# Loading each adjacency chunk of a two-layer GNN kernel by sixteen DMAs of four row blocks in place of four DMAs of a whole quadrant

## What is computed

```python
A = adj + eye(4096)                      # layer 0
d = rsqrt(sum(A, axis=1))
A_hat = A * d[:, None] * d[None, :]
x1 = layernorm(x + elu((A_hat @ x) @ w))
out = layernorm(x1 + relu((adj @ x1) @ W.T + b))   # layer 1
```

## Time and profile before

| | |
|---|---|
| runs | 949.61, 950.19, 953.15 us (median 950.19) |
| span of the profiled execution, first to last instruction | 945.9 us |
| median less that span (lies around it) | 4.3 us |
| TensorE busy / VectorE / ScalarE / GpSimd | 798.6 / 736.0 / 530.9 / 101.9 us |
| read from HBM | 185.2 MB |
| DMAs of `adj` / of `x` | 336 of 512 KB / 64 of 128 KB |

### The profile page before, as it was taken

One profiled execution on the slowest core, in us unless ns is written; L12 is line 12 of the kernel. 1 busy time (PEld: TensorE's weight loads), 2 busy tenths in 40 slices (PEclk: granted clock), 3 DMA queues, 4 the chain that ended last, 5 costly groups with the idle time before them and its releaser, 6 DMA issues. The chain is left out here.

```text
span 945.9 us, 10551 instructions
## 1 busy us (share of the span) xinstructions
PE 798.6 (84%) x3524; PEld 656.8 (69%) x3524; DVE 736.0 (78%) x537; ACT 530.9 (56%) x1192; POOL 101.9 (11%) x108
## 2 busy tenths in 40 slices
PE   0151756569989999999999999999999999999993
PEld 0041635457768888888888888888887778888882
DVE  0454636579979878989898898988987979888861
ACT  2153535367777764475676757667573665455352
POOL 0000000000000000021110211202110231122020
PEclk9995777788999999999999999999999999999997
DMA  9999999999999999998999999999999799998900
GB/s 215 221 219 221 221 220 220 221 225 238 228 230 227 203 206 216 208 219 180 199 209 197 201 207 193 212 191 220 195 211 212 171 211 209 219 219 181 198 23 22
DMA packets 191972, 190.08 MB, mean 201 GB/s; under 512 B 6960, under 2 KB 191920, under 8 KB 191920
## 3 DMA queue, kind: packets, MB, share of 16 engines
q1 hardware_dynamic: 187312, 185.23, 96.2%
q10 hardware_dynamic: 4608, 4.20, 1.5%
HBM read 185.20 MB, written 4.19 MB: 200 GB/s over the span
## 5 line engine op out<-in xcount | busy, mean ns | idle before, releaser
L710 PE MATMUL acc<-a_hi,v_hi 128*128 128x512 f32 x1024 | 411.7, 402 | 35.6 <-DVE a_lo L496 31.4
L343 ACT ACTIVATE a_hi<-turned 128x1024 fp32r<-128x1024 f32 x256 | 265.2, 1058 | 309.5 <-DVE turned L479 151.6
L711 PE MATMUL acc<-a_lo,v_hi 128*128 128x512 f32 x1024 | 406.3, 397 | 0.0
L712 PE MATMUL acc<-a_hi,v_lo 128*128 128x512 f32 x1024 | 406.0, 396 | 0.0
L479 DVE STREAM_TRANSPOSE turned<-raw 128x2048 f32<-128x2048 f32 x128 | 294.1, 2305 | 85.2 <-DMA raw<-in_adj_dram 78.6
L496 DVE TENSOR_TENSOR a_lo<-turned,a_hi 128x1024 fp32r<-128x1024 f32 x256 | 301.4, 1215 | 23.4 <-ACT a_hi L343 15.0
L710 PEld LDWEIGHTS acc<-a_hi,v_hi 128*128 128x128 f32 x1024 | 197.3, 193 | 80.3 <-issue 28.7
L712 PEld LDWEIGHTS acc<-a_hi,v_lo 128*128 128x128 f32 x1024 | 196.9, 192 | 42.3
L711 PEld LDWEIGHTS acc<-a_lo,v_hi 128*128 128x128 f32 x1024 | 197.4, 193 | 40.7
L353 ACT ACTIVATE acc<-raw 128x256 f32<-128x256 f32 x236 | 86.8, 368 | 47.1 <-DMA raw<-in_adj_dram 47.1
L503 DVE TENSOR_REDUCE deg_parts<-raw 128x10 f32<-128x2560 f32 (+4 forms) x32 | 78.1, 2444 | 27.0 <-DMA raw<-in_adj_dram 27.0
(11 more groups left out here) (43 smaller groups left out, 347.3 us busy)
## 6 DMA issues: line engine op xcount, KB each, us to landing
raw<-in_adj_dram SPq DMA_DIRECT2D x336, 512.0 KB, 10.4
x_row<-in_x_dram SPq DMA_DIRECT2D x64, 128.0 KB, 9.3
out_dram<-normed ACTq DMA_DIRECT2D x32, 128.0 KB, 2.7
w_sb<-in_L_gnn_w_dram SPq DMA_DIRECT2D x1, 256.0 KB, 12.4
normed<-in_L_gnn_W_dram SPq DMA_DIRECT2D x1, 256.0 KB, 10.7
b_sb<-in_L_gnn_b_dram SPq DMA_DIRECT2D x1, 128.0 KB, 10.1
```

Source lines behind the costliest of these rows:

```text
L343: nc.scalar.activation(a_hi[u % 2][:, part, :], turned[u % 2][:, part, :], ACT.Copy).then_inc(s_hi, 1)
L710: pe.matmul(dst, v_hi[:, k, ch], a_hi[u % 2][:, t, :], start=begin, stop=False)
L711: pe.matmul(dst, v_hi[:, k, ch], a_lo[u % 2][:, t, :], start=False, stop=False)
L712: ins = pe.matmul(dst, v_lo[:, k, ch], a_hi[u % 2][:, t, :], start=False, stop=end)
```

## The change

A constant `BLOCKS = 4` is added. A chunk is now loaded by sixteen DMAs, each of one quadrant and four of its row blocks: 32 partitions x 4 blocks x 1 KB = 128 pieces, 128 KB. The outer loop runs over the blocks, the inner one over the quadrants 0, 2, 1, 3. The pieces are the same 1 KB, the bytes the same; `raw_loaded` waits for 256 instead of 64 a chunk. `load_x`, the weights and every other engine's instructions are as before.

```diff
+    BLOCKS = 4
@@
         def load_chunk(eng, n, qs):
             _, row, panel, _ = chunks[n]
-            for q in qs:
-                eng.dma_start(raw[buffer_of[n]][B32 * q:B32 * (q + 1), :, :], adj_part(row, panel, q)).then_inc(s_raw[buffer_of[n]], 16)
+            for first in range(0, RB, BLOCKS):
+                some = slice(first, first + BLOCKS)
+                for q in qs:
+                    eng.dma_start(raw[buffer_of[n]][B32 * q:B32 * (q + 1), some, :],
+                                  adj_part(row, panel, q)[:, some, :]).then_inc(s_raw[buffer_of[n]], 16)
@@
         def raw_loaded(eng, n):
-            eng.wait_ge(s_raw[buffer_of[n]], 64 * filled[n])
+            eng.wait_ge(s_raw[buffer_of[n]], 16 * STRIPES * (RB // BLOCKS) * filled[n])
```

## The result

The changed kernel takes 912.07 us (median of 4 runs, 908.08 to 914.45) against 951.67 us for the kernel before (with a fourth run, 949.61 to 953.61): ratio 0.959, 95% interval 0.956 to 0.962. It is faster, and by twice what was forecast: 39.6 us in place of 19 to 20. The predicted range began at 914 us, 2 us above the measured median.

A forecast was written before the change was run, and what follows sets the result against it. Loads were taken to bound groups 0 to 4, and TensorE the time after 313 us. Savings of 16.1 us there, 3 us in groups 5 to 7 and 1 us in B and C made 19 to 20 us: 931 us, range 914 to 951.

The forecast's parts named there:

- What bounds the kernel: Loads at 220 GB/s set the pace to 196 us, loads and TensorE the next 117 us, TensorE afterwards.
- The mechanism: Loads: at a change of half some engines are in each half, raising the rate; sixteen DMAs make four times as many changes.
- The new rate: Load stream of groups 0 to 4: 240 GB/s instead of 220, saving 16.1 us.
- the peak of the swing: Steady load stream: the rate swings once per DMA, from 209 or 211 GB/s to 233 or 236 at its peak.
- the upper bound: New load rate: at most 260 GB/s, half the bytes at 343 and half at the trough's 210.
- Can SP feed it: SP's issuing: sixteen DMAs take 7.6 or 9.1 us a chunk, against 8.7 us of transfer at 240 GB/s.
- The rivals with SP as the pace: Part A: SP keeps the old pace, 946 to 953 us, chance 0.08; or is slower, 962 to 990 or more, chance 0.13.
- more than I think: Groups 0 to 4: only SP limits, 7.6 us a chunk, 276 GB/s, 39 us saved, near 905 us; chance 0.06.
- Groups 5 to 7: From 196.4 us, for the next 117 us: a quarter of TensorE's 12.0 us idle time is gained, 3 us.
- Parts B and C: After 313 us: loads stay covered by TensorE's 10.7 us a chunk; 1 us added for places where they aren't.
- Completion writes: DMA engines: 16128 more small packets, nothing added to the sum; upper bound 0.9 us a chunk.
- The rule quoted against a gain: Skill text: two DMAs on different halves run one after the other, +6% over one; strictly, the rate stays 220 GB/s.

The follow-up runs named there:

- part A alone: The changed kernel with four blocks a DMA in part A only, whole quadrants in parts B and C: 914.37 us, ratio 0.960.
- B and C alone: The changed kernel with whole quadrants in part A, four blocks a DMA only in parts B and C: 948.93 us, ratio 0.9965.
- the probe: Loads without arithmetic, fourteen stages varying blocks, quadrant order and queues: 220 GB/s for the old form, 260 for the new, 345 with whole quadrants on two queues.

## Why the prediction was wrong

**What bounds the kernel** was right, though in the earlier trace rows the twelfth slice of TensorE reads 8, not 9. The gain lies in part A, groups 0 to 4 above all; part A alone gives 914.37 us, B and C alone 948.93.

**The mechanism** was right: changes of half raise the rate. The order 0, 1, 2, 3 takes back two thirds, and quadrants 0 and 1 alone never leave 205 GB/s. The half was an assumption there; the probe shows it now. The picture behind it, engines in both halves at once, is still an inference.

**The new rate** is the step that failed, by its size. "I take 240, between that peak and 247": the stream ran at 265 GB/s over the first 180 us, and 193 x (1 - 220/265) = 32.8 us, against 32.9 us measured and 16.1 forecast. From 240 to 265 it lacked 25 GB/s, in four parts. First, the worth of a change: in time, 220 and 229 GB/s are 2.38 and 2.29 us per 512 pieces, 0.09 us for a change, from three short windows over `x` loads; the probe has 0.12, which makes 260 of four changes, 10 more than 0.09 would. Second, "I take 240": I took the peak of the swing, 233 to 236 GB/s in windows of half a microsecond, for a ceiling and went 7 GB/s below my own 247. Such a window is longer than the 0.12 us that a change saves, and mixes it with what lies beside it. Third, the kernel's own stream ran 5 GB/s above the probe's 260, which nothing here explains. Fourth and least, 3 GB/s, I added rates (9 GB/s a change), where it is times that add: with 0.09 us a change four of them give 250 and not 247. And the upper bound came from a model of my own, engines spread over both halves for half of the time; its 260 is what the probe shows as the ordinary rate.

**Can SP feed it:** right. 0.432 us and a gap of 0.04, 7.6 us a chunk, and its waits shrank. The rivals with SP as the pace at 9.1 us a chunk or more, 0.08 and 0.13, had their price from the 0.526 us of `x` issues; the new form's median is 0.432. The rival "more than I think" had this pace, 276 GB/s, with a chance of 0.06 and 905 us; group 1 ran at 277. The measured 912 us lies between it and the forecast's lower end. With the SP limit known from rows, the range should have reached to it.

**Groups 5 to 7:** 5.3 us for the 3 of the sum, of 12.0 at most. **Parts B and C:** 1.4 us in the profiled executions and 3 us by the run of those parts alone, for 1. The "about 1 us of latency" there is too small: of the four issues from 588.0 to 589.4 us the first landed 4.4 us after its start, 2.4 us of which is the transfer, so about 2. The load of 8.7 us and 2 stays near TensorE's 10.7, and the term came out small all the same. **Completion writes:** nothing to be seen at 128 pieces. With two changes per 512 pieces and twice the DMAs the probe has 228 GB/s against 230, the kernel 236 against 232.

**The rule quoted against a gain.** One queue with alternating halves moves 260 GB/s against 205 for one half (plus 27%), and two queues 345. The Trainium skill's sentence (SBUF — State Buffer, "Can I just issue two DMAs to hit both halves?") does not hold here: one transfer over all 128 partitions isn't the only way to use both halves. What its section on the port swizzle says of the halves, eight ports each, is borne out: 203 and 205 GB/s in the two stages whose loads all lie in one half, 343 to 345 when both are written at once.

**What stays open:** why the same sixteen DMAs run at 277 GB/s in one stretch, 261 in another, 260 alone and 252 in another kernel. The lag between engines may depend on what came before; no run fixed it. Of two queues in part A the packets say that one half runs alone in 38 of 150 us; which wait leaves it alone each time (a buffer that is not free, the projection, the `x` loads, ACT's own work) I did not separate, though a buffer refilled one chunk late costs 10 us. And 865 us with a quarter of the loads against 898 says that some 33 us of loading are left in part A.

## What to carry to other kernels

Where loads must go by quadrants of 32 partitions, alternate the halves (0, 2, 1, 3) in DMAs as small as the issuing queue can afford, about 0.475 us each; count the changes of half and add their savings as times, not as rates. Better still, give each half its own queue, with packets of one size, on an engine whose own work doesn't hold up the refill, and only in the stretch that waits for loads; here that was ACT in part A, and not GpSimd. When an unknown rate carries the whole forecast, let the range reach to the next hard limit that the rows show, here the issuing queue's, and not to a model of the unknown.

## What the runs showed of the hardware

DMAs of 512 KB on two queues, one for each half of the partitions, ran at 345 GB/s, 57% above the 220 of the same DMAs on one queue, and as fast as the 343 of loads that span all partitions. Both queues on the same half gave 203. On one queue each change of half saved 0.12 us of 2.50 us per 512 KB. GpSimd's queue moved packets of 4 KB where SP's and ACT's moved 1 KB, and beside SP's queue it took about four fifths of the bytes (200 to 212 GB/s against 48 to 55). DMAs of 64 pieces cost SP as much as those of 128: 0.427 and 0.432 us.
